# A transformer block over 256 groups of windows: the hardware loop replaced by straight code

## The reference

```python
x = _L0_conv_ref(x, ...)                       # windowed attention (7x7, shifted, 8 heads) + MLP 64->256->64
t = _to_tokens(x)
t = t + _L1_attn_ref(_ln_t(t), ...)            # linear attention per image, 16 heads of 4 channels
t = t + _L1_ffn_ref(_ln_t(t), ...)             # 8 experts 64->256->64, the two best per token, weighted
```

## Time and profile before

| | |
|---|---|
| median of 3 runs | 8549.95 us (8541.93 to 8550.66) |
| the profiled execution's own time | 8553.12 us |
| its span, first to last instruction | 8551.3 us |
| TensorE busy in the span | 7998.7 us (94%) |
| VectorE, ScalarE, GpSimd busy | 78%, 73%, 54% |
| mean granted clock of TensorE | 0.984 |

### The profile page before, as it was taken

The page is one execution under the profiler, slowest core; times in us unless marked ns, Lnnn a source line. Parts: engine busy times, 40 slices in busy tenths (PEclk is TensorE's granted clock), DMA queues, the critical chain, the costliest instruction groups (busy, mean ns, idle before and its releaser), DMA issues. The chain is left out here.

```text
span 8551.3 us, 254939 instructions
## 1 busy us (share of the span) xinstructions
PE 7998.7 (94%) x77810; PEld 5197.8 (61%) x77810; DVE 6646.8 (78%) x26070; ACT 6253.5 (73%) x10999; POOL 4618.5 (54%) x7940
## 2 busy tenths in 40 slices
PE   6799999999999999999999999999999999999987
PEld 5566666666666666666666666666666666666652
DVE  4467788878887888878888888888888788788762
ACT  2367777777777777777777777777777777777764
POOL 1245555555555555555555555555555555555542
PEclk9999999999999999999999999999999999999998
DMA  0001111111111111111111111111111111111111
GB/s 23 4 25 30 35 31 35 35 35 35 31 35 35 35 35 32 35 35 35 31 35 35 35 32 35 35 35 33 33 36 35 34 32 35 36 35 31 35 28 40
DMA packets 216035, 281.52 MB, mean 33 GB/s; under 512 B 30372, under 2 KB 214217, under 8 KB 214345
## 3 DMA queue, kind: packets, MB, share of 16 engines
q1 hardware_dynamic: 214600, 264.20, 10.9%
HBM read 235.04 MB, written 28.90 MB: 31 GB/s over the span
## 5 line engine op out<-in xcount | busy, mean ns | idle before, releaser
L1281 ACT ACTIVATE ht<-ps,be 128x392 f32<-128x392 f32 x4096 | 2346.6, 586 | 561.3 <-PE ps L697 344.4
L707 PE MATMUL ps<-ht,we 128*64 128x392 f32 x8192 | 1587.7, 509 | 17.9 <-DVE yg L1035 17.6
L697 PE MATMUL ps<-xs,we_hi 128*128 128x392 f16 x4096 | 1384.3, 338 | 97.4 <-ACT ht L1281 96.1
L697 PE MATMUL ps<-xs,we_lo 128*128 128x392 f16 x4096 | 1358.7, 332 | 0.0
L1088 POOL TENSOR_TENSOR sc<-sc,mx 113x392 f32<-113x392 f32 x1024 | 916.4, 905 | 429.1 <-DVE mx L872 429.1
L697 PEld LDWEIGHTS ps<-xs,we_hi 128*128 128x128 f16 x4096 | 407.2, 99 | 880.7 <-issue 535.4
L707 PEld LDWEIGHTS ps<-ht,we 128*64 128x64 f32 x8192 | 501.7, 137 | 698.8 <-issue 617.2
L1105 POOL TENSOR_TENSOR kvsd<-kvsd,cs 98x128 f32<-98x128 f32 x256 | 102.5, 400 | 1328.9 <-ACT kvsd L1247 1328.9
L1074 POOL TENSOR_TENSOR rs<-ve,cs 98x4 f32<-98x4 f32 x768 | 790.7, 1030 | 21.4
L1174 ACT ACTIVATE pt<-ps 98x392 f32<-98x392 f32 x1024 | 513.6, 502 | 320.6 <-PE ps L557 302.2
L1035 DVE SCALAR_TENSOR_TENSOR yg<-ps,be,gb 128x392 f32<-128x392 f32 x1024 | 625.3, 611 | 121.7 <-DMA gb<-gates 63.8
(11 more groups left out here) (185 smaller groups left out, 19025.9 us busy)
## 6 DMA issues: line engine op xcount, KB each, us to landing
gb<-gates SPq DMA_DIRECT2D x1024, 196.0 KB, 3.7
xg<-in_x SPq DMA_DIRECT2D x256, 98.0 KB
out_y<-yo SPq DMA_DIRECT2D x256, 98.0 KB
gates<-gtt SPq DMA_DIRECT2D x256, 12.2 KB
bias<-in_rel SPq DMA_DIRECT2D x1, 1200.5 KB
bias<-in_w SPq DMA_DIRECT2D x2, 512.0 KB
gb<-in_amask SPq DMA_DIRECT2D x2, 300.1 KB
we<-in_w SPq DMA_DIRECT2D x1, 512.0 KB
```

What stands on the lines that cost most here:

```text
L697: last = pe.matmul(pH[b % 2][:, 0:GTOK], we1[half][:, 128 * b:128 * (b + 1)], xs[:, g.j % 2, :], start=(half == 0), stop=(half == 1))
L707: last = pe.matmul(pY[C * e:C * (e + 1), 0:GTOK], we2[:, b, :], ht[:, b % 8, :], start=(h == 0), stop=(h == 1), skip_group_check=True)
L1281: act.activation(ht[:, b % 8, :], pH[b % 2][:, 0:GTOK], ACT.Gelu, bias=be1[:, b:b + 1], scale=1.0 / WSCALE).then_inc(S["h_ready"], 1)
```

## The change

Both limits of the loop are set to the number of bodies, so that no turn is left: the condition `tail > head` is false, the loop and its counter are not made, and all 256 groups come from the first line that calls `iteration`, as straight code with integers.

```diff
             bodies = TOTAL // BODY
-            head = min(2, bodies)
-            tail = max(bodies - 1, head)
+            head = bodies
+            tail = bodies
             for n in range(-LEAD, BODY * head):
                 iteration(0, n, n, n)
             if tail > head:
```

## The result

| | us | ratio to before, 95% interval |
|---|---|---|
| before, median of 4 runs | 8545.94 (8530.71 to 8550.66) | |
| straight code, median of 4 runs | 8950.33 (8930.43 to 8990.34) | 1.0487 [1.0467, 1.0506] |
| predicted | 8932 (8840 to 9010) | |

What follows compares the result with a forecast made beforehand. TensorE, busy 94%, was taken to bound the kernel. 8551 - 73 (jumps) + 208 (waits) + 250 (clock) = 8936 us, adjusted from the profiled execution to the median: 8932 us, 4.5% more; range 8840 to 9010 us.

Steps and rivals of the forecast that it cites:

- What bounds the kernel: TensorE, busy 94% of the span; written-out groups of the kernel before, 33.37 us each against the loop's 31.53, show its new period.
- The jumps: At the loop's turns TensorE stops and then runs slower, 6.1 us a turn; removing 12 gives back 73 us.
- The waits: In softmax_exp, GpSimd's late wait moves ahead of exp's table load, delaying qs and fc11: about +1.0 us a group, +208 us.
- the gap: TensorE's idle wait for qs before step fc11, 1.10 us in a written-out group, put at about +1.0 us a group.
- The clock: With the idle wait in every group, TensorE falls to 1.2 GHz in some: +1.2 us a group, +250 us.
- At no cost: instructions and fetching: Register instructions leave every queue and straight code asks for no more fetching than the loop: given nothing.
- falls belong to the ends of the program: First rival: clock falls occur only at the program's ends, steady period 32.2 us, some 8690 us; chance 0.05.
- only the jumps count: Second rival: the table load stands ahead of the late wait as in the loop, 8477 us; chance 0.03.
- Falls in every second group: Third rival: clock falls become more frequent, 3.2 us a group, period 35.4 us, 9350 us; chance 0.10.

Runs made afterwards that it cites:

- run 3: The kernel before, loop kept, with softmax_exp's two waits exchanged in its written-out bodies alone: 8455.94 us, ratio 0.9904 to before.
- run 1: The straight kernel with softmax_exp's two waits exchanged, so that exp's table load stands behind the early wait: 8389.91 us, ratio 0.9825 to before.
- run 2: The kernel before, loop kept, with softmax_exp's late wait made an instruction of its own ahead of the table load in the loop: 9086.97 us, ratio 1.0652.
- run 6: The straight kernel, late wait kept, with 3 extra matmuls ahead of fc11's wait in every group: 8621.15 us, ratio 1.0096 to before.

## Why the prediction was right

*What bounds the kernel.* Right. The written-out stretches of before were a sample of the kernel to come: their mean of 33.37 us a group stands against 33.63 in the profiled execution. That one is the slowest of four runs; the median, 18 us above the prediction, asks for a period of some 33.5 us (18 / 208 = 0.09 more than 33.37), within the spread of the four runs.

*The jumps.* Predicted 73 us from two periods around a turn, measured 66 us (run 3 to run 1). The stops at line 569 went with the loop. The rule of the Trainium skill (Runtime: NRT & Kernel Launch, "Instruction fetch mechanics"), that a taken branch to code outside the fetched window costs a stall and that kernels therefore prefer full unrolling, agrees with the stops at the jumps (38.8 us in run 3, none in run 1) and is outweighed here.

*The waits.* Right in mechanism, and shown: exchanging two waits removes the gap in straight code (run 1), and a late wait ahead of the load makes it in the loop (run 2). The gap alone is run 6 (three extra matmuls) against run 1, 8621.15 - 8389.91 = 231 us in 256 groups, 0.90 us each, where 1.0 was predicted.

*The clock.* Predicted 1.2 us a group by difference. The straight kernel against run 6 gives 8950.33 - 8621.15 = 329 us, 1.29 us each (1.21 to 1.44 by the fastest and the slowest of its four runs). So the gap was put 0.10 us too high and the clock 0.09 us too low. That the two cancel is not evidence for the split: the clock's share was taken as what the gap left of a measured period, so the sum could hold whatever the split. For the 208 groups that changed, 208 x (0.90 + 1.29) - 66 = 390 us, of the 404 measured; some 14 us stay open, less than the spread of the straight kernel's runs (60 us).

*At no cost: instructions and fetching.* Right in the time. Run 1 fetches straight code too, runs at a clock of 1.00 without the stops, and its period is 31.16 us (line 1043, 209 periods from 1259.4 to 7772.8 us), no longer than the 31.18 us of the loop without turns. The straight kernel fetched 10.53 + 4.29 MB for 231720 instructions, 64 bytes each. One reading was wrong: the loop's groups do wait for issue elsewhere, a little in each at line 507. Run 1 waits there for longer, 0.49 us against 0.30, and its period shows no cost of it. The loop of before, then the whole of run 1:

```profile
PE ps L507 <- issue: 61.9, 207, 0.3
...
PE ps L507 <- issue: 116.2, 237, 1.7
```

*The rivals.* That falls belong to the ends of the program is refuted by the clock of 0.95 over the former loop. That only the jumps count, the side of a faster kernel, is what run 1 shows for the case that was its condition, an early load; the change itself did not have it. Falls in every second group would have cost 3.2 us a group, where they cost 1.29.

## What to carry to other kernels

Where a table load stands ahead of an activation, look which wait stands ahead of the load: a late one takes its cover away. Which wait that is can change with the form of the waits though the source lines stay, and it can differ between two steps of the same form: exp and the square root in the loop of before. Read it from the idle time before each load. A kernel that already contains a stretch in the changed form is its own sample; read its period, not its reasons, first. Behind an idle instruction count the waits for everything in the same queue after it, not only for its own result.

## What was not expected of the hardware

Three matmuls whose results nobody reads made the kernel 3.7% faster (8950 to 8621 us), because with an idle gap of TensorE cut from 1.10 to 0.45 us its clock no longer fell from 2.4 to 1.2 GHz. Run 1 shows that the clock holds without added work once the gap is gone; whether in the run with 3 the shorter gap or the added work holds it, the runs do not part. The fall cost more than the gap: 1.29 us a group on the mean against 0.90 us.
